# A two-layer graph network on one core: edge rows issued side by side in time, a shorter last sum, an earlier mixing of the first block

## The reference, cut to what matters

```
edge_index = stack([src, dst])                    # 1250 nodes, 41250 edges, 512 features
h = relu(layernorm(x));  x = x + L0(h)            # degree-normalised sum of h @ W.T + b over the edges
h = relu(layernorm(x));  x = x + L1(h)

# L1, the part that this case is about: 16 segments of 32 features, 64 paths (i1, i2, i3)
x1 = h[src].reshape(-1, 16, 32)                   # rows of the source nodes, gathered
x2 = edge_attr.reshape(-1, 16, 32)                # rows of the edges, 84 MB, read once
contrib  = path_coeffs[None, :, None] * x1[:, i1, :] * x2[:, i2, :]
edge_out = zeros(E, 16, 32).at[:, i3, :].add(contrib)
out      = zeros(N, 512).at[dst].add(edge_out)
```

## Time and profile before

| what | value |
|---|---|
| time before, median of 3 runs | 1072.91 us (1070.64 to 1081.23) |
| the profiled execution | 1072.47 us, span of its instructions 1070.8 us |
| busy: VectorE, TensorE, GpSimd, ScalarE | 897.5, 829.7, 492.3, 444.3 us |
| mean granted TensorE clock | 0.878 of full speed |
| DMA | 183.03 MB, mean 171 GB/s |
| first product of turn 0, last of turn 11 | at 292.15 and 1054.51 us |

### The profile page before, as it was taken

How to read it: one execution, slowest core, us unless ns; L and a number is a source line. 1 busy time by engine, 2 the same in 40 slices (tenths; PEclk the granted TensorE clock), 3 DMA queues, 4 the chain that set the end, 5 groups by cost and what they waited for, 6 DMA issues and landing times.

```text
span 1070.8 us, 22798 instructions
## 1 busy us (share of the span) xinstructions
PE 829.7 (77%) x5046; PEld 394.0 (37%) x5053; DVE 897.5 (84%) x2196; ACT 444.3 (41%) x1685; POOL 492.3 (46%) x572
## 2 busy tenths in 40 slices
PE   1688887996167787868788987878797787887878
PEld 0343443442022443524243443424344243443426
DVE  4677668843069999999999999899998999999894
ACT  3888887432401523425161432416133261522423
POOL 4211220443634546566454657546564564646400
PEclk9999999998578898898889888888987889888788
DMA  9000000043555656687665657666565775767610
GB/s 166 1 0 0 0 0 2 15 192 124 165 229 204 229 177 238 233 284 249 240 239 187 235 195 275 255 219 245 188 233 195 254 256 182 247 188 241 225 21 10
DMA packets 59517, 183.03 MB, mean 171 GB/s; under 512 B 20116, under 2 KB 20244, under 8 KB 54972
## 3 DMA queue, kind: packets, MB, share of 16 engines
q0 software_dynamic: 27616, 87.97, 26.1%
q1 hardware_dynamic: 22568, 88.88, 22.3%
q10 hardware_dynamic: 9268, 5.55, 1.9%
HBM read 173.71 MB, written 8.66 MB: 170 GB/s over the span
## 4 chain that ended last, share of the span: by engine, by line
PE 26%; DVEq 21%; DVE 20%; issue 17%; ACT 6%; POOL 4%; DMA 2%; ACTq 1%; SPq 1%; another core or an unknown queue 1%; POOLq 0%
DVE q_mem L858 16%; PE psum L1226 15%; DVEq L850 10%; DVEq L853 5%; PE psum L1211 4%; DVEq L858 4%; PE psum L1129 3%; ACT S L1059 3%; PE psum L1140 2%; DVE x_mem L748 2%; ACT hot_mem L1046 2%; DMA x_mem<-in_L_gnn_W 1%; PE psum L1126 1%; POOL x_mem L622 1%; POOL spare L515 1%
## 5 line engine op out<-in xcount | busy, mean ns | idle before, releaser
L858 DVE TENSOR_TENSOR q_mem<-x_mem 128x448 f32 (+2 forms) x1392 | 725.6, 598 | 68.3 <-DMA x_mem<-h_rows,src_now 31.6
L1226 PE MATMUL psum<-q_mem,hot_mem 128*32 128x512 f32 x2584 | 424.4, 714 | 136.6 <-DVE q_mem L858 79.4
L622 POOL DMA_INDIRECT x_mem<-h_rows,src_now x323 | 390.8, 1210 | 174.3 <-issue 94.5
L1059 ACT ACTIVATE S<-psum,coef 128x32 f32<-128x32 f32 (+1 forms) x800 | 147.5, 335 | 301.4 <-issue 133.6
L1226 PEld LDWEIGHTS psum<-q_mem,hot_mem 128*32 128x32 f32 x2584 | 107.5, 126 | 414.5 <-issue 294.1
L1211 PEld LDWEIGHTS psum<-S,place 128*128 128x128 f32 x1600 | 187.8, 194 | 45.9 <-issue 45.7
L1211 PE MATMUL psum<-S,place 128*128 128x32 f32 x1600 | 195.2, 278 | 11.8 <-issue 11.5
L748 DVE TENSOR_SCALAR x_mem<-x_mem,spare 128x320 bf16<-128x320 f16 x323 | 77.8, 299 | 42.0 <-issue 42.0
L1071 ACT ACTIVATE acc<-psum 128x512 f32<-128x512 f32 x12 | 7.2, 597 | 201.4 <-PE psum L1211 201.4
L1140 PE MATMUL psum<-x_mem,hot_mem 128*128 128x320 bf16 x323 | 67.2, 321 | 28.8 <-DVE x_mem L748 20.3
L953 ACT ACTIVATE hot_mem<-x_mem,spare 128x128 bf16<-128x128 f16 x240 | 74.9, 388 | 20.5 <-PE psum L1140 20.0
(11 more groups left out here) (187 smaller groups left out, 437.8 us busy)
## 6 DMA issues: line engine op xcount, KB each, us to landing
x_mem<-in_edge_attr SPq DMA_DIRECT2D x60, 768.0 KB
x_mem<-in_edge_attr SPq DMA_DIRECT2D x35, 1024.0 KB
x_mem<-h_rows,src_now POOLq DMA_INDIRECT x323
out<-acc POOLq DMA_DIRECT2D x12, 256.0 KB, 4.3
x_mem<-in_x SPq DMA_DIRECT2D x1, 2304.0 KB
out<-x_mem ACTq DMA_DIRECT2D x9, 256.0 KB
h_rows<-x_mem ACTq DMA_DIRECT2D x9, 256.0 KB, 2.0
x_mem<-in_L_gnn_W SPq DMA_DIRECT2D x1, 1024.0 KB, 13.9
```

The source lines that it names most:

```text
L622: pool.indirect_dma_start(x1[:, j * TB + t, :], None, h2_dram[:, :], bass.IndirectOffsetOnAxis(ap=now, axis=0)).then_inc(landed, 16)
L858: return nc.vector.tensor_tensor(q[s % 2][:, 0:tiles, p % PG:p % PG + 1, :], x1_segs[:, first:first + tiles, ds(a, 1), :], x2_segs[:, firs ...
L1059: last = nc.scalar.activation(S[:, p * U:(p + 1) * U], sums, ACT.Copy, scale=coef[:, p:p + 1])
L1226: last = nc.tensor.matmul(ps[s % G][side * M:(side + 1) * M, :], hot[:, j * TB + k, :], q[s % 2][:, k, :, :].rearrange("p n u -> p (n u)") ...
```

## The change

It has five parts. (1) In `load`, the DMAs of sides 2 and 3 of a batch each wait for one more slot of VectorE: for batch 1 slots 0 and 1 of the running turn, for batch 0 of the next turn slots 4 and 5 of the running one. The last turn's loads stay. (2) In the late block TensorE sums only the first EDGE = 10 of the 16 positions (320 columns in place of 512); the other six are summed, by matmuls of their own ahead of it, only where more than 58 positions are kept. (3) Block 0 is mixed behind slot 4 instead of slot 5, in all turns. (4) VectorE reads the count of the next turn's loop behind slot 4 of the running turn, instead of ahead of the loop. (5) TensorE reads `n_kept` once.

```diff
+    EDGE = 10
-    MIX_AT, MIX_LAST = {1: [G - 1], 0: [G - 2], G + 1: [0], 2 * G - 1: [1]}, {1: [G - 1], 0: [G - 2], G + 1: [0], G + 2: [1]}
+    MIX_AT, MIX_LAST = {1: [G - 1], 0: [G - 2], G: [0], 2 * G - 1: [1]}, {1: [G - 1], 0: [G - 2], G: [0], G + 2: [1]}
...
                     for s in range(S4):
                         if j == 0 and s == EARLY:
                             sp.wait_ge(agg_summed, C)
+                        if s >= 2:
+
+                            sp.wait_ge(multiplied, group(turn, s - 2) if j else group_before(turn, G + s - 2))
...
-            def product_turn(again, turn):
+            def product_turn(again, turn, next_item):
                 for j in range(2):
...
                     for g in range(G):
                         product_slot(turn, j * G + g, g, j * TB, n)
+                        if j and g == 0:
+                            many_next = item_turn_count(next_item)
+                return many_next
...
-            for item in range(ITEMS - 1):
-                product_turns(dve, item, turn_count, product_turn)
-            product_turns(dve, ITEMS - 1, turn_count, product_last)
+            def item_turn_count(item):
+                return dve.value_load(meta[0:1, TURNS + item:TURNS + item + 1], min_val=1, max_val=WINDOWS * PLACES)
+
+            many = item_turn_count(0)
+            for item in range(ITEMS):
+                with dve.Fori(0, many) as again:
+                    turn = dve.snap(turn_count, min_val=0, max_val=ITEMS * WINDOWS * PLACES - 1)
+                    if item < ITEMS - 1:
+                        many_next = product_turn(again, turn, item + 1)
+                    else:
+                        product_last(again, turn)
+                    dve.reg_add(turn_count, turn_count, 1)
+                many = many_next
...
+            kept_n = pe.value_load(n_kept, min_val=SURE, max_val=NP)
...
-                for t in range(max(b - a for a, b in cut)):
-                    for side, (a, b) in enumerate(cut):
-                        if t < b - a:
-                            k = at[side] + t
-                            last = nc.tensor.matmul(ps[s % G][side * M:(side + 1) * M, :], hot[:, j * TB + k, :],
-                                                    q[s % 2][:, k, :, :].rearrange("p n u -> p (n u)"),
-                                                    start=(j == 0 and t == 0), stop=(j == 1 and t == b - a - 1))
-                last.then_inc(summed, 1)
+
+                def add(first, end):
+                    for t in range(max(b - a for a, b in cut)):
+                        for side, (a, b) in enumerate(cut):
+                            if t < b - a:
+                                k = at[side] + t
+                                last = nc.tensor.matmul(ps[s % G][side * M:(side + 1) * M, first * U:end * U], hot[:, j * TB + k, :],
+                                                        q[s % 2][:, k, first:end, :].rearrange("p n u -> p (n u)"),
+                                                        start=(j == 0 and t == 0), stop=(j == 1 and t == b - a - 1))
+                    return last
+
+                if s % G < G - 1:
+                    add(0, PG).then_inc(summed, 1)
+                else:
+                    with pe.If(kept_n > NP - PG + EDGE):
+                        add(EDGE, PG)
+                    add(0, EDGE).then_inc(summed, 1)
```

## The result

The changed kernel is **slower: 1134.49 us, median of 4 runs (1128.81 to 1141.17), against 1071.85 us before (four runs by now); ratio 1.0567, 95% interval 1.0474 to 1.0659.** Ratios in this document leave out executions that took over 1.5% longer than the fastest of their kernel, medians do not. I had forecast slower, 1096 us with a range up to 1112. The direction and the place were right; the size was not. The profiled execution took 1128.8 us (span 1127.1; before 1070.8).

The account below looks back on a forecast made before the run. VectorE was taken as the bound. From 1072.5 us, moving block 0's mixing adds 35 (3.2 us a turn, eleven turns) and staggered edge rows take off 11.5: 1096 us, own range 1085 to 1106, 8 in 10 for 1070 to 1112.

Parts of the forecast that it names:

- what bounds the kernel: VectorE, busy 302.37 of 307.62 us in turns 1 to 5; the change can give back only its idle time.
- The ten positions at no gain: Sums of slots 3 and 7 fall from 3.63 to 2.3 us, under cover: nothing in a turn, 1 us at the end.
- the edge rows in time: Last side issued some 14 us before needed, takes 3.7, cover 10 us; rival of late rows, 2 us over: 1140, chance 0.04.
- clearing and mixing take 599.93 to 604.00 = 4.07: TensorE in turn 4, behind the save: block 0's clearing and mixing keep 4.07 us, moved to 597.9 to 602.0.
- no longer its own: Slot 5's sum, after 7.1 us without a sum, resembles slot 0's case: 5.86 us taken, between ends of 3.63 and 6.55.
- slot 4's sum: TensorE ahead of the save: 6.3 us taken against an average of 5.9, since the pause ahead of it grows.
- from there to VectorE's product: From the end of slot 5's sum to slot 7's product: 0.55 us, read from slot 6's sum ahead of slot 0.
- wait ahead of slot 7: VectorE in turn 4: slot 7 waits for slot 5's sum and begins at 608.4 instead of 604.4, 4.0 us later.
- turn 11 at nothing: Last turn: mixing fills TensorE's 3.04 us pause ahead of slot 5; slower clock set against the shorter last sum: 0.
- relief of 11.5 us: Staggered edge rows halve the DMA burst: 4.5 us less in turn 0, 7 less in turns 6, 8 and 11 together.
- rival (a): Edge-row DMA bursts are moved and not relieved, gaps last as long as the bytes fly: 1107 us, chance 0.17.
- Rival (c): Slot 5's sum runs at full clock directly behind the mixing, turn drops to 61.1: 1045 us, chance 0.10.

Follow-up runs that it names:

- mix_only: Kernel before with nothing but block 0 mixed behind slot 4 instead of slot 5: 1128.34 us, ratio 1.0815.
- mix_back: Changed kernel with block 0 mixed behind slot 5 again, all else kept: 1054.26 us, ratio 1.0099 to the kernel before.
- edge_only: Kernel before with nothing but the edge rows issued one side at a time: 1046.28 us, ratio 0.9999.
- edge_ten: Kernel before with the staggered edge rows and the ten positions, old mixing order and old place of the count: 1055.03 us, ratio 0.9971.
- second set: Runs on one other chip; the kernel before, unchanged, took 1047.58 us there, the changed kernel, unchanged, 1125.11 us, ratio 1.0753.
- no_pause: Changed kernel mixing block 2's saved sums of the turn before behind slot 4, without waiting for the save; block 0 left out: 1072.26 us, ratio 1.0124.
- fill_mix: Changed kernel with six unneeded matmuls in the pause for the save and one behind every fourth matmul of block 0's mixing: 1114.82 us, ratio 1.0510.
- after_fill: Changed kernel with four unneeded matmuls on TensorE between slot 4's sum and the wait for the save: 1109.07 us, ratio 1.0617 to the kernel before.

## Why the prediction was right and wrong

**Right: what bounds the kernel and where the loss stands.** VectorE was the bound. The wait moved from slot 0 (10.5 us to 1.8) to slot 7 (0.1 to 71.8), in every turn, released by slot 5's sum behind the save and the mixing. mix_only and mix_back show the moved mixing to be nearly the whole loss. The ten positions at no gain, slot 3's sum at 2.35 us (2.3 forecast) in all turns; slot 7's is at 2.35 in four turns only and 3.4 to 4.5 in the other eight, at a low clock that I had not reckoned with, but under its cover. The branch and, alone, the count at nothing; the edge rows in time everywhere.

**Wrong: the term "clearing and mixing take 599.93 to 604.00 = 4.07".** I carried a duration from a place where the clock was up to one where, by my own argument for slot 5's sum ("no longer its own" case), it is down. This is the step of the forecast that failed: the mixing measured 5.5 to 7.0 us, with its clearing 6.5 on average. The terms of one turn, forecast and measured (means of turns 0 to 10 of the changed kernel):

| term | forecast | measured |
|---|---|---|
| slot 4's sum | 6.3 | 5.5 |
| standing for the save | 3.0 | 3.2 |
| clearing and mixing | 4.1 | 6.5 |
| slot 5's sum, to its release | 5.86 | 5.75 |
| from there to VectorE's product | 0.55 | 1.1 |
| wait ahead of slot 7 | 4.0 in turn 4 (slot 4's sum 6.55), 3.8 with it at 6.3 | 5.9 |

The mixing is 2.4 us of the difference, some 27 us in eleven turns. The 0.55 from sum to product was also taken from another place: ahead of slot 0 there are no branches, ahead of slot 7 the sequencer runs five compare-and-branch instructions once the wait is over (499.48 to 500.82 in turn 2). That is another 6 us. Slot 4's sum gave 9 us back. Slot 5's sum itself, for which I had looked for a likeness and found slot 0's 5.86, came out at 5.75; that the mean met it so closely is luck, since single turns have 4.8 to 6.4. The same care for the mixing would have given 1120 and more.

**Wrong: turn 11 at nothing.** I had the mixing fill the pause of 3.04 there. TensorE stands 3.17 for the save in its place, the mixing takes 7.04, slot 7 waits 6.4, and the end behind the last product is 2.4 longer.

**Wrong: the relief of 11.5 us from the staggered edge rows.** edge_only measures 0.9999 (0.9979 to 1.0020). Turn 0 of the changed kernel has its gaps inside slots still, 9.1 us against 9.9; so has edge_ten on another chip (9.2), and other profiles have none with or without the staggering. In these gaps VectorE's sequencer takes some 0.7 us for register operations that take 0.06 to 0.28 elsewhere; what holds it up no run shows. Two rows of the changed kernel's turn 0, for the earlier trace rows:

```profile
301.75 0.63 DVE L863 TENSOR_TENSOR q_mem<-x_mem 128x448 f32 x1 [1.42 <-issue]
303.88 0.62 DVE L863 TENSOR_TENSOR q_mem<-x_mem 128x448 f32 x1 [1.50 <-issue]
```

So rival (a) was right in this part: moved, not relieved. The rule of the Trainium skill that I had weighed ("DMA: Bandwidth & Descriptors", section "Queues, rings and completion order", that an engine goes round its queues packet by packet) is in agreement with that, though no run here isolates it. Turns 6, 8 and 11 did lose their excess in the changed kernel's profile (13.5 to 2.7 us ahead of slots 1 to 3), but the kernel before has no such turns in the second set either, so nothing is shown by it.

**The range** ended at 1112 since its upper rival (a) added nothing to the mechanism itself. With the mixing doubled as at half the clock (an estimate; no row of before has a mixing at 0.50) and the longest of each other term (6.5, 3.0, 7.4, 6.5, 0.55) the turn is 68.8 and the time above 1140: that bound could be worked out before the run.

**Rival (c)** asked for slot 5's sum at full clock behind the mixing. Even without the pause it takes 5.33 in the turn shown and 3.6 to 6.3 in all (no_pause), and with it 4.8 to 6.4; only among fillers (fill_mix) is it fast. Nothing in the changed kernel keeps the clock up there.

## What to carry to other kernels

When a step is moved behind a wait, no duration behind that wait may be taken over from the old place: each TensorE term is to be priced at the clock of the new place, the small matmuls of a bookkeeping step as much as the large ones. An in-order queue that has something useful to do while another engine saves its result hides two things, the save and the clock; here three microseconds of standing cost six to six and a half. Long turns in one profile are no pool from which a change can be paid, as long as a second profile of the same kernel hasn't shown them.

## What the runs showed of the hardware that I had not expected

- Thirty-two records of 128x32 matmuls with their fp32 weight loads took 3.76 us wherever the profile before shows block 0's mixing, and 7.04 at a granted clock of 0.50. The mean of all weight loads of that line went from 194 to 231 ns (busy 187.8 to 227.5 us).
- Adding work made TensorE's queue faster: after_fill, four more matmuls in each pause, 1109 against 1125 us in the same set. It held the clock in no turn; with more fillers, and some among the small matmuls (fill_mix), it held in nine of twelve.
- The length of a pause alone does not tell what the sum behind it takes. Slot 5's sum took 3.63 behind 3.30 us and 5.33 behind 3.31 (mix_back, turns 2 and 10); in the kernel before it took 3.63 behind 3.14 (turn 5) and 5.33 behind 1.97 (turn 9).
- The same kernel took 1045 us in one set and 1072 in another. Part of it is gaps in turn 0: 9 to 10 us inside slots in seven of the seventeen profiles, 5.6 in one, next to none in the other nine.
- From the end of its wait to its product VectorE takes 0.5 to 0.6 us ahead of slot 0 and 1.0 to 1.35 ahead of slot 7, with five branches in between.
